# Partial shifts of the first convolution in tiles of 64 and 32 columns, with float32 weights laid out as a band

## Chip, core and metric

The kernel runs on one core of a Trainium2 chip. Every time here is in microseconds of that core (device time); a kernel is stated by the median of its runs. PE is TensorE (PEld its weight loads), DVE VectorE, ACT ScalarE, POOL GpSimd, SP the engine that issues most DMAs.

## What is computed

For 32 samples of 128 channels by 2048 positions the kernel applies four residual layers in float32. The first and the last are grouped convolutions (4 groups of 32 channels, 9 taps), the two between mix the channels with a matrix that depends on the sample.

```python
def _L0_cond_ref(x, c, weight, c_weight, bias):
    out = lax.conv_general_dilated(x, weight, window_strides=(STRIDE,), padding=[(PAD, PAD)],
                                   dimension_numbers=('NCH', 'OIH', 'NCH'), feature_group_count=GROUPS)
    ctx = jnp.einsum('nd,od->no', c, c_weight)
    out = out + ctx[:, :, None] + bias[None, :, None]
    return out
...
def _L1_cond_ref(x, embedding, W0, b0, W1, b1, W2, b2, weight, bias_k):
    ...
    att = jax.nn.softmax((h @ W2 + b2) / T, axis=-1)
    agg_w = jnp.einsum('bk,koi->boi', att, weight[..., 0])
    agg_b = att @ bias_k
    out = jnp.einsum('boi,bih->boh', agg_w, x) + agg_b[:, :, None]
    return out
...
x = x + _L0_cond_ref(x, cond_128, L0_cond_weight, L0_cond_c_weight, fside_S_0)
x = x + _L1_cond_ref(x, cond_128, ...)
x = x + _L2_cond_ref(x, cond_128, ...)
x = x + _L3_cond_ref(x, cond_128, L3_cond_weight, L3_cond_c_weight, fside_S_0)
```

## The kernel before

The 2048 positions of a sample are split into four phases (PH = 4, position modulo 4) of S = 512. For one group g, the 32 input channels stand in 32 partitions (`rows(g)`, one of PE's four row groups), and the four output phases times 32 output channels make 128 output columns of the array. With 9 taps and 4 phases there are SHIFTS = 12 shifts d. A shift reads phase `d % PH` of the input, moved by `d // PH` positions (`c`), and gives to output phase p the tap d - p, where that lies between 0 and 8. Six of the shifts (WHOLE, d = 3 to 8) reach all four phases. The other six (d = 0, 1, 2 and 9, 10, 11) reach some of them: the first three only the phases p <= d, the last three only the phases p > d - 9.

Float32 products come in two ways. The whole shifts are done in float32r, three times: high part of the taps by high part of x, low by high, high by low (`x_hi`, `x_lo`, `taps_hi`, `taps_lo`), each as a matmul of 32 rows by 128 columns that streams 512 columns of data (`whole_turns`, L1079). The partial shifts of samples 2 to 31 are done in plain float32, once, from `x_full` and `taps_raw`: `partial_turns` (L1090) makes three turns (PARTIAL = 3), n = 0, 1, 2. In a turn it issues for each group and each phase one tile of 32 rows by 32 columns: phase p takes shift n if p <= n, else shift n + 9. So d = n and d = n + 9 together fill the 128 columns, and a turn has 16 tiles, each at its own place of the array; PSUM bank g takes group g. Each float32 matmul is run by the chip in two passes. The first two samples use float32r for all shifts (`conv0`).

`conv0_mixed` is what a sample's first convolution is: whole turns with waits on `x_hi_done`, `x_lo_done` and the edges, for sample 2 also a product (`middle`), and then the partial turns. The last turn's matmuls count up `conv0_done` once a group; ScalarE (`high_y`, L639) and VectorE (`low_y`, L836) then take the banks. PE's order of work is written out by hand in `one`: the first convolution of sample b, the last convolution of sample b - 1 (L1068) with the small product for sample b + 1 (L1185, later L1192) in its midst, then the mix of sample b (L1214). The steady part is a loop of two samples a turn; 30 samples, 2 to 31, have partial turns.

`taps_raw[0]` is made by VectorE in the setup (L910, L913: a transpose, and the identity added for the residual), [channel of the group, tap, output channel]. `taps_raw_step[0]` reaches 2 when it is ready. GpSimd's program after the setup memsets is `spread_first` (two kinds of DMA issues, L560 and L563, which wait for the first product), `first_planes` (L527), and then one copy into phases of x (L496) and one weave of the output (L513) for each sample.

Of the kernel before, what the change touches and what calls it, by code (L numbers as in the profile page):

```python
# [30 lines left out]
N, C, L = 32, 128, 2048  # L31
G = 4
GC = C // G
# [10 lines left out]
WHOLE = [*range(PH, 2 * PH), PH - 1, 2 * PH]  # L44
PARTIAL = PH - 1
FIRST_MIXED = 2
K = 8
D = 128
DMA = 16
# [11 lines left out]
def conditioned_residual_kernel(nc, x, cond, side, conv0_w, ctx0_w, mix1, mix2, conv3_w, ctx3_w, out):  # L61
# [9 lines left out]
    with ctx:  # L71
        def sb(name, shape, dt=F32):
            return ctx.enter_context(nc.sbuf_tensor(name, shape, dt))
# [16 lines left out]

        taps_hi = [sb(f"taps_hi{l}", [C, SHIFTS, C], F32R) for l in range(2)]
        taps_lo = [sb(f"taps_lo{l}", [C, SHIFTS, C], F32R) for l in range(2)]
        mix1_w = sb("mix1_w", [C, K, C])
        mix2_wT = sb("mix2_wT", [C, K, C])
        mat1 = sb("mat1", [C, C])
# [71 lines left out]
        of_group_done = sem("of_group_done")  # L167
        taps_zeroed = [sem(f"taps_zeroed{l}") for l in range(2)]
        taps_raw_step = [sem(f"taps_raw_step{l}") for l in range(2)]
        taps_hi_done = [sem(f"taps_hi_done{l}") for l in range(2)]  # L170
        taps_lo_done = [sem(f"taps_lo_done{l}") for l in range(2)]
        mlp_rows_in = sem("mlp_rows_in")
# [315 lines left out]
        def _(pool):  # L488
# [91 lines left out]
                pool.memset(buf[:, :, ROW - 1:ROW].bitcast(F32), 0.0).then_inc(far_zeroed, 1)  # L580
            for buf in x_full:
                pool.memset(buf[:, :, 0:ROW:ROW - 1], 0.0).then_inc(far_zeroed, 1)
            spread_first()
            first_planes(ALL[1], 1)
            for t in ALL[2:N]:
# [474 lines left out]
        def _(pe):  # L1060
# [18 lines left out]
                        pe.matmul(ps[:, first_bank + g, :], w[rows(g), d, :], a[rows(g), d % PH, c:c + S],  # L1079
                                  start=(first and (k, d) == turns[0]), stop=False)  # L1080

            def partial_turns(first_bank, l, full, done, step):


                for n in range(PARTIAL):
                    for g in range(G):
                        for p in range(PH):
                            d = n if p <= n else n + TAPS
                            c = step * (d // PH)
                            tile = pe.matmul(ps[rows(p), first_bank + g, :], taps_raw[l][rows(g), d - p, :],  # L1090
                                             full[rows(g), d % PH, c:c + S], start=False, stop=(n == PARTIAL - 1))
                        if n == PARTIAL - 1:
                            tile.then_inc(done, 1)

            def conv0_mixed(t, middle=None):
                b = t.i
                hi, lo, full = x_hi[t.par(0)], x_lo[t.par(0)], x_full[t.par(0)]
                step = 1 if plain(t, 0) else BLK
                near, far = WHOLE[:PH], WHOLE[PH:]
                pe.wait_ge(x_hi_done, b + 1)  # L1100
                if t.at(N - 1):
                    pe.wait_ge(plain_ends, 3)
                wait(pe, out_act, 2 * (b - 1))
                wait(pe, out_dve, 2 * (b - 1))
                whole_turns(bank(t, 0), 0, hi, lo, [(k, d) for k in range(2) for d in near], step, True)
                if not plain(t, 0):
                    pe.wait_ge(x_hi_edged, b + 1 - PLAIN)
                whole_turns(bank(t, 0), 0, hi, lo, [(k, d) for k in range(2) for d in far], step, False)
                if not plain(t, 0):
                    pe.wait_ge(x_full_edged, b + 1 - PLANED)  # L1110
                pe.wait_ge(x_lo_done, b + 1)
                whole_turns(bank(t, 0), 0, hi, lo, [(2, d) for d in near], step, False)
                if not plain(t, 0):
                    pe.wait_ge(x_lo_edged, b + 1 - PLAIN)
                whole_turns(bank(t, 0), 0, hi, lo, [(2, d) for d in far], step, False)
                if middle:
                    middle()
                partial_turns(bank(t, 0), 0, full, conv0_done, step)

            def conv0(t, turns=range(TURNS)):  # L1120
                b = t.i
# [280 lines left out]
```

## Time and profile before

| | us |
|---|---|
| median of 3 runs | 632.58 (632.04 to 632.8) |
| profiled execution, its own time | 635.33 |
| its span, from the first to the last instruction | 633.5 |
| PE busy | 622.8 (98%) |
| DVE busy | 500.9 (79%) |
| ACT busy | 338.2 (53%) |
| POOL busy | 272.3 (43%) |

The profile is one execution. A busy time is the time in which an engine has at least one instruction in work; on PE several run at once in different places of the array, so that counts times durations exceed it. Ends of matmuls are modelled, their starts are read. The median above is of other executions than the profiled one.

### The profile page before, as it was taken

The page shows a single profiled execution, that of the slowest core. Times are in us where ns is not written, and L with a number is a line of the kernel's source. Part 1 is how long each engine was busy: PE and PEld are TensorE (multiplying, and loading weights), DVE is VectorE, ACT ScalarE, POOL GpSimd, SP SyncE. Part 2 cuts the span into 40 slices and gives each one's busy share as a digit, 9 for nine tenths or more (in the row PEclk, how much of TensorE's full clock was granted, in tenths as well). Part 3 has the DMA queues.
Part 4 walks back from the last instruction along what each step waited for, and adds up shares of the span by engine and source line. Part 5 has one row for each costly group of instructions (what it writes and reads, how often), then busy time and mean ns, then how long its engine had stood idle before and what let it go on. Part 6 is the DMA issues. An engine that isn't in the chain of part 4 may idle for free.

```text
span 633.5 us, 26750 instructions
## 1 busy us (share of the span) xinstructions
PE 622.8 (98%) x11938; PEld 506.3 (80%) x11938; DVE 500.9 (79%) x1002; ACT 338.2 (53%) x626; POOL 272.3 (43%) x163
## 2 busy tenths in 40 slices
PE   8999999999999999999999999999999999999995
PEld 6888897777788777889877778777878877788874
DVE  6899777978777887887887887797877788788735
ACT  4665455555455456455456446555545545645534
POOL 4133454354355345355435345435435534534220
PEclk8999999999999999999999999999999999999998
DMA  8066665557765556775555776555776555655515
GB/s 244 24 188 215 203 211 177 204 163 225 232 207 156 190 176 199 232 232 158 173 191 175 232 232 182 158 202 162 223 232 208 155 190 176 201 169 168 161 76 201
DMA packets 50572, 118.84 MB, mean 188 GB/s; under 512 B 5621, under 2 KB 26282, under 8 KB 42714
## 3 DMA queue, kind: packets, MB, share of 16 engines
q1 hardware_dynamic: 49170, 116.04, 58.1%
q0 software_dynamic: 576, 1.26, 0.5%
q10 hardware_dynamic: 776, 0.89, 0.4%
q8 instruction: 30, 0.49, 0.3%
q14 instruction: 20, 0.16, 0.1%
HBM read 35.33 MB, written 33.55 MB: 109 GB/s over the span
## 4 chain that ended last, share of the span: by engine, by line
PE 96%; DMA 2%; DVE 1%; ACT 1%; issue 0%; ACTq 0%; DVEq 0%
PE ps L1068 45%; PE ps L1079 19%; PE ps L1090 16%; PE ps L1214 14%; PE ps L1192 1%; DMA out_sb<-in_L_cond_weight 1%; DMA out_planes<-out_taps 1%; ACT out_sb L740 1%; PE ps L1262 0%; PE ps L1185 0%; DVE out_taps L856 0%; DVE x_in L950 0%; DVE x_hi L993 0%; PE ps L1250 0%; PE ps L1302 0%
## 5 line engine op out<-in xcount | busy, mean ns | idle before, releaser
L513 POOL COPY out_sb<-out_planes 128x2048 f32<-128x2048 f32 x30 | 123.0, 4099 | 187.8 <-issue 162.0
L496 POOL COPY x_full<-x_in 128x2048 f32<-128x2048 f32 x29 | 117.1, 4038 | 113.9 <-DVE x_lo L822 110.1
L846 DVE SCALAR_TENSOR_TENSOR z_lo<-ps,bias_tab,z_hi 128x1024 fp32r<-128x1024 f32 x62 | 76.7, 1279 | 60.7 <-ACT z_hi L649 60.7
L1090 PE MATMUL ps<-x_full,taps_raw 32*32 32x512 f32 x2880 | 102.2, 598 | 0.0
L1068 PEld LDWEIGHTS ps<-z_hi,taps_hi 32*128 32x128 f32 x1488 | 71.0, 183 | 35.4 <-issue 25.1
L1068 PE MATMUL ps<-z_hi,taps_lo 32*128 32x512 f32 x1488 | 96.5, 387 | 0.0
L836 DVE SCALAR_TENSOR_TENSOR y_lo<-ps,bias_tab,y_hi 128x512 fp32r<-128x512 f32 x128 | 87.2, 744 | 10.2 <-ACT y_hi L639 10.2
L1068 PE MATMUL ps<-z_hi,taps_hi 32*128 32x512 f32 x1488 | 94.2, 396 | 0.0
L657 ACT ACTIVATE out_taps<-ps,bias_tab 128x512 f32<-128x512 f32 x62 | 39.3, 685 | 102.2 <-PE ps L1068 102.2
L1068 PE MATMUL ps<-z_lo,taps_hi 32*128 32x512 f32 x1488 | 90.3, 385 | 0.0
L1214 PE MATMUL ps<-y_hi,mix_w 32*128 32x512 f32 x1024 | 88.0, 385 | 0.0
L649 ACT ACTIVATE z_hi<-ps,bias_tab 128x1024 fp32r<-128x1024 f32 x62 | 65.8, 1113 | 34.2 <-PE ps L1214 34.2
L1068 PEld LDWEIGHTS ps<-z_lo,taps_hi 32*128 32x128 f32 x1488 | 77.9, 183 | 6.9
L639 ACT ACTIVATE y_hi<-ps,bias_tab 128x512 fp32r<-128x512 f32 x128 | 77.0, 683 | 9.9 <-PE ps L1090 7.6
L1068 PEld LDWEIGHTS ps<-z_hi,taps_lo 32*128 32x128 f32 x1488 | 75.1, 183 | 6.1
L1090 PEld LDWEIGHTS ps<-x_full,taps_raw 32*32 32x32 f32 x2880 | 42.1, 103 | 43.2 <-issue 35.6
L822 DVE TENSOR_TENSOR x_lo<-x_full,x_hi 128x2048 fp32r<-128x2048 f32 x31 | 70.8, 2284 | 0.0
L601 ACT ACTIVATE x_hi<-x_full 128x2048 fp32r<-128x2048 f32 x30 | 57.9, 1931 | 2.0 <-POOL x_full L527 2.0
L898 DVE TENSOR_REDUCE prod_sum<-ps 128x128 f32<-128x1024 f32 (+2 forms) x31 | 35.4, 1143 | 29.3 <-PE ps L1192 24.3
L1214 PEld LDWEIGHTS ps<-y_hi,mix_w 32*128 32x128 f32 x1024 | 53.9, 183 | 4.7 <-DVE y_lo L836 0.3
L691 ACT ACTIVATE mat_hi<-mat 128x128 fp32r<-128x128 f32 x27 | 8.4, 311 | 91.1 <-DVE mat L875 91.1
L1214 PE MATMUL ps<-y_lo,mix_w 32*128 32x512 f32 x512 | 52.9, 385 | 0.0
(158 smaller groups left out, 831.0 us busy)
## 6 DMA issues: line engine op xcount, KB each, us to landing
x_in<-in_x SPq DMA_DIRECT2D x31, 1024.0 KB, 5.3
out_planes<-out_taps SPq DMA_DIRECT2D x122, 256.0 KB, 3.6
out<-out_sb SPq DMA_DIRECT2D x30, 1024.0 KB, 4.6
mix_w<-prod SPq DMA_DIRECT2D x124, 128.0 KB, 4.0
x_in<-in_x SPq DMA_DIRECT2D x2, 512.0 KB, 5.9
out<-out_sb POOLq DMA_DIRECT2D x2, 512.0 KB, 3.5
out<-x_full SPq DMA_DIRECT2D x7, 128.0 KB, 2.9
out_taps<-in_L_cond_weight SPq DMA_DIRECT2D x1, 512.0 KB, 5.8
```

The costliest lines, as they stand in the source:

```text
L496: pool.tensor_copy(row_order(t, d, x[:, :, home(t, d)]), x_order(t, d, x_in[t.par(d)][:, :])).then_inc(x_planed, 1)
L513: pool.tensor_copy(x_order(t, d, out_sb[t.par(d)][:, :]), row_order(t, d, out_planes[:, :, :]))\
L601: act.activation(x_hi[p][:, :, home(t, d)], x_full[p][:, :, home(t, d)], ACT.Copy).then_inc(x_hi_done, 1)
L639: act.activation(y_hi[:, g, :], ps[:, bank(t, 0) + g, :], ACT.Identity, bias=bias_tab[:, b, g:g + 1]).then_inc(y_hi_done, 1)
L649: act.activation(z_home(t, 0)[0][:, 2 * h:2 * h + 2, home(t, 0)], ps[:, k:k + 2, :], ACT.Identity, bias=bias_tab[:, b, 2 * G:BIAS]).then_i ...
L822: dve.tensor_tensor(out=x_lo[p][:, :, home(t, d)], in0=x_full[p][:, :, home(t, d)], in1=x_hi[p][:, :, home(t, d)].bitcast(F32), op=ALU.sub ...
L836: dve.scalar_tensor_tensor(out=y_lo[:, g, :], in0=ps[:, bank(t, 0) + g, :], scalar=bias_tab[:, b, g:g + 1], in1=y_hi[:, g, :].bitcast(F32) ...
L846: dve.scalar_tensor_tensor(out=z_home(t, 0)[1][:, 2 * h:2 * h + 2, home(t, 0)], in0=ps[:, k:k + 2, :], scalar=bias_tab[:, b, 2 * G:BIAS], ...
L1068: tile = pe.matmul(ps[:, first_bank + g, :], w[rows(g), d, :], a[rows(g), d % PH, c:c + S], start=(n == 0), stop=(n == TURNS - 1))
L1079: pe.matmul(ps[:, first_bank + g, :], w[rows(g), d, :], a[rows(g), d % PH, c:c + S], start=(first and (k, d) == turns[0]), stop=False)
L1090: tile = pe.matmul(ps[rows(p), first_bank + g, :], taps_raw[l][rows(g), d - p, :], full[rows(g), d % PH, c:c + S], start=False, stop=(n == ...
L1214: tile = pe.matmul(ps[:, bank(t, 0) + p, :], w[rows(p), g, h, :], a[rows(p), g, :], start=(n == 0), stop=(n == 3 * G - 1))
```

## The change

`TILES` lists for each turn the tiles as (shift, first phase, end phase). Neighbouring phases that take the same shift are joined where two of them make a tile of 64 columns that starts at column 0 or 64; the others stay at 32 columns. With four groups a turn has 12, 8 and 12 matmuls instead of 16 each. A tile of 64 columns needs the taps of both phases side by side: `taps_full` holds, for each of the six partial shifts, the 128 columns with the taps of the phases that the shift reaches and zeros elsewhere. GpSimd fills it once, with a memset and six copies, behind its setup memsets; PE waits for it ahead of sample 2.

```diff
+TILES = (((0, 0, 1), (9, 1, 2), (9, 2, 4)), ((1, 0, 2), (10, 2, 4)), ((2, 0, 2), (2, 2, 3), (11, 3, 4)))
...
+            pool.memset(taps_full[:, :, :], 0.0).then_inc(taps_full_zeroed, 1)
+            pool.wait_ge(taps_full_zeroed, 1)
+            pool.wait_ge(taps_raw_step[0], 2)
+            for p in range(PH):
+                if p < PARTIAL:
+                    last = pool.tensor_copy(taps_full[:, p:PARTIAL, rows(p)], taps_raw[0][:, 0:PARTIAL - p, :])
+                if p > 0:
+                    last = pool.tensor_copy(taps_full[:, PARTIAL:PARTIAL + p, rows(p)], taps_raw[0][:, TAPS - p:TAPS, :])
+            last.then_inc(taps_full_done, 1)
             spread_first()
...
-                for n in range(PARTIAL):
+                for n, tiles in enumerate(TILES):
                     for g in range(G):
-                        for p in range(PH):
-                            d = n if p <= n else n + TAPS
-                            c = step * (d // PH)
-                            tile = pe.matmul(ps[rows(p), first_bank + g, :], taps_raw[l][rows(g), d - p, :],
-                                             full[rows(g), d % PH, c:c + S], start=False, stop=(n == PARTIAL - 1))
-                        if n == PARTIAL - 1:
+                        for d, p, q in tiles:
+                            c, o = step * (d // PH), slice(GC * p, GC * q)
+                            tile = pe.matmul(ps[o, first_bank + g, :], taps_full[rows(g), d if d < PARTIAL else d - TAPS + PARTIAL, o],
+                                             full[rows(g), d % PH, c:c + S], start=False, stop=(n == len(TILES) - 1))
+                        if n == len(TILES) - 1:
                             tile.then_inc(done, 1)
...
+                if t.at(FIRST_MIXED):
+                    pe.wait_ge(taps_full_done, 1)
```

PE's order at the partial turns of sample 2, before the change. A row is a run of like matmuls with the columns of the array by the columns streamed, and their count:

```order
L1079 MATMUL ps<-x_lo,taps_hi 128x512 x24
L1185 MATMUL ps<-mat2T,mat 128x128 x4
L1090 MATMUL ps<-x_full,taps_raw 32x512 x48
L1068 MATMUL ps<-z_hi,taps_hi 128x512 x48
L1068 MATMUL ps<-z_hi,taps_lo 128x512 x40
```

The same place of the changed program (L1092, L1199, L1102 and L1081 are the lines that were L1079, L1185, L1090 and L1068):

```order
L1092 MATMUL ps<-x_lo,taps_hi 128x512 x24
L1199 MATMUL ps<-mat2T,mat 128x128 x4
L1102 MATMUL ps<-x_full,taps_full 32x512 x2
L1102 MATMUL ps<-x_full,taps_full 64x512
...
L1102 MATMUL ps<-x_full,taps_full 32x512 x2
L1102 MATMUL ps<-x_full,taps_full 64x512 x10
L1102 MATMUL ps<-x_full,taps_full 32x512 x2
L1102 MATMUL ps<-x_full,taps_full 64x512
...
L1102 MATMUL ps<-x_full,taps_full 32x512 x2
L1081 MATMUL ps<-z_hi,taps_hi 128x512 x48
```

One run of 48 tiles of one size has become 15 runs that alternate between 32 and 64 columns (eight of two tiles, six of one, one of ten), and this is so for each of the 30 samples.

GpSimd's order in the setup, before the change, with the waits named:

```order
L582 MEMSET x_full 128x4x2 x2
L560 DMA mix_w<-prod 32x4x128 [waits prod_hi_done]
L563 DMA mix_w<-prod 32x4x128 [waits prod_lo_done]
L563 DMA mix_w<-prod 32x4x128
L527 COPY x_full<-x_in 128x4x8x32 [waits x_lo_done,z_hi_done,x_hi_done,x_loaded0]
```

And in the changed program:

```order
L586 MEMSET x_full 128x4x2 x2
L587 MEMSET taps_full 128x768
L592 COPY taps_full<-taps_raw 128x3x32 [waits taps_raw_step0,taps_full_zeroed]
L592 COPY taps_full<-taps_raw 128x2x32
L594 COPY taps_full<-taps_raw 128x32
L592 COPY taps_full<-taps_raw 128x32
L594 COPY taps_full<-taps_raw 128x2x32
L594 COPY taps_full<-taps_raw 128x3x32
L564 DMA mix_w<-prod 32x4x128 [waits prod_hi_done]
```

The memset and the six copies stand ahead of the first DMA issue that waits for the product.

## Rows read from the trace of the kernel before

**Rows 1.** The page: busy time of each engine, granted TensorE clock in 40 slices
```profile
PE 622.8 (98%) x11938; PEld 506.3 (80%) x11938; DVE 500.9 (79%) x1002; ACT 338.2 (53%) x626; POOL 272.3 (43%) x163
...
PEclk8999999999999999999999999999999999999998
```

**Rows 2.** The page: chain that ended last, shares of the span by line
```profile
PE ps L1068 45%; PE ps L1079 19%; PE ps L1090 16%; PE ps L1214 14%; PE ps L1192 1%; DMA out_sb<-in_L_cond_weight 1%; DMA out_planes<-out_taps 1%; ACT out_sb L740 1%; PE ps L1262 0%; PE ps L1185 0%; DVE out_taps L856 0%; DVE x_in L950 0%; DVE x_hi L993 0%; PE ps L1250 0%; PE ps L1302 0%
```

**Rows 3.** That chain from 290 to 345: by line; start, us, what
```profile
by line: PE ps L1068 43.9%; PE ps L1079 22.2%; PE ps L1090 18.2%; PE ps L1214 14.8%; PE ps L1192 1.3%
...
301.51 3.33 PE ps L1090 x91
...
320.33 3.33 PE ps L1090 x91
```

**Rows 4.** Groups by line and shape, PE: rows*columns, count | busy us, mean ns
```profile
L1090 PE MATMUL ps<-x_full,taps_raw 32*32 32x512 f32 x2880 | 102.2, 598 | 0.0
...
L1068 PE MATMUL ps<-z_lo,taps_hi 32*128 32x512 f32 x1488 | 90.3, 385 | 0.0
```

**Rows 5.** Timeline around 301.4: start, us, engine, line, shapes, count [idle before]
```profile
301.13 0.38 PE L1079 MATMUL ps<-x_lo,taps_hi 32*128 32x512 f32 x1
...
301.44 0.24 PEld L1090 LDWEIGHTS ps<-x_full,taps_raw 32*32 32x32 f32 x32 [0.35 <-issue]
```

**Rows 6.** Timeline within the stretch: five short windows between 302.1 and 303.9
```profile
301.90 0.69 PE L1090 MATMUL ps<-x_full,taps_raw 32*32 32x512 f32 x16
...
302.33 0.89 PE L1090 MATMUL ps<-x_full,taps_raw 32*32 32x512 f32 x7
...
302.33 0.37 PEld L1090 LDWEIGHTS ps<-x_full,taps_raw 32*32 32x32 f32 x11 [0.32 <-issue]
...
302.52 0.18 PEld L1090 LDWEIGHTS ps<-x_full,taps_raw 32*32 32x32 f32 x10
...
303.20 1.22 PE L1090 MATMUL ps<-x_full,taps_raw 32*32 32x512 f32 x17
```

**Rows 7.** Timeline around 304.8, where the stretch ends
```profile
304.05 0.81 PE L1090 MATMUL ps<-x_full,taps_raw 32*32 32x512 f32 x14
...
304.26 0.59 PE L1090 MATMUL ps<-x_full,taps_raw 32*32 32x512 f32 x1
304.78 0.50 PE L1068 MATMUL ps<-z_hi,taps_hi 32*128 32x512 f32 x4
...
304.78 0.30 PEld L1068 LDWEIGHTS ps<-z_hi,taps_hi 32*128 32x128 f32 x8 [0.84 <-issue]
```

**Rows 8.** Timeline around 56.3, first such stretch, behind the product
```profile
56.04 0.27 PE L1185 MATMUL ps<-mat2T,mat 32*128 32x128 f32 x1
56.24 0.70 PE L1090 MATMUL ps<-x_full,taps_raw 32*32 32x512 f32 x14
```

**Rows 9.** Timeline around 83.9, float32 product and float32r convolution, one size
```profile
83.85 0.53 PEld L1068 LDWEIGHTS ps<-z_hi,taps_lo 32*128 32x128 f32 x9
...
83.88 0.28 PE L1185 MATMUL ps<-mat2T,mat 32*128 32x128 f32 x3
```

**Rows 10.** Timeline of POOL, 0 to 62
```profile
0.74 0.52 POOL L540 MEMSET y_hi<- 128x512 f32 x1 [0.29 <-POOLq L1388]
...
28.56 0.58 POOL L560 DMA_DIRECT2D mix_w<-prod  x1 [21.17 <-DVE prod L901]
...
45.14 0.79 POOL L531 COPY x_full<-x_full 128x189 f32<-128x189 f32 x2
```

**Rows 11.** The chain in order of time, near its start
```profile
8.31 1.10 DVE x_hi L993
```

**Rows 12.** Windows: stretch, length, busy us (count) PE PEld DVE ACT POOL, clock, DMA
```profile
6.00:8.00 2.00, 1.10 (x4) 0.62 (x4) 1.50 (x3) 0.76 (x4) 1.39 (x11) 1.00 1.05 310
...
11.00:12.00 1.00, 1.00 (x13) 0.84 (x16) 0.90 (x3) 0.87 (x3) 0.00 (x0) 0.57 1.23 352
...
17.00:18.00 1.00, 1.00 (x20) 0.91 (x16) 0.28 (x1) 0.00 (x0) 0.00 (x0) 0.52 0.08 16
```

More of the change, by code:

```diff
@@ L92, in conditioned_residual_kernel @@
         taps_lo = [sb(f"taps_lo{l}", [C, SHIFTS, C], F32R) for l in range(2)]
+        taps_full = sb("taps_full", [C, 2 * PARTIAL, C])
         mix1_w = sb("mix1_w", [C, K, C])
@@ L169, in conditioned_residual_kernel @@
         taps_raw_step = [sem(f"taps_raw_step{l}") for l in range(2)]
+        taps_full_done = sem("taps_full_done")
+        taps_full_zeroed = sem("taps_full_zeroed")
         taps_hi_done = [sem(f"taps_hi_done{l}") for l in range(2)]
@@ L1080, in whole_turns, with partial_turns @@
                                   start=(first and (k, d) == turns[0]), stop=False)
-            def partial_turns(first_bank, l, full, done, step):
-                for n in range(PARTIAL):
+            def partial_turns(first_bank, full, done, step):
+                for n, tiles in enumerate(TILES):
                     for g in range(G):
-                        for p in range(PH):
-                            d = n if p <= n else n + TAPS
-                            c = step * (d // PH)
-                            tile = pe.matmul(ps[rows(p), first_bank + g, :], taps_raw[l][rows(g), d - p, :],
-                                             full[rows(g), d % PH, c:c + S], start=False, stop=(n == PARTIAL - 1))
-                        if n == PARTIAL - 1:
+                        for d, p, q in tiles:
[3 more added lines that the diff above has]
+                        if n == len(TILES) - 1:
                             tile.then_inc(done, 1)
@@ L1117, in conv0_mixed @@
                     middle()
-                partial_turns(bank(t, 0), 0, full, conv0_done, step)
+                partial_turns(bank(t, 0), full, conv0_done, step)
             def conv0(t, turns=range(TURNS)):
```

## Prediction

> **What bounds the kernel now.** I read the page's busy times first: TensorE (PE) is busy 622.8 of 633.5 us, VectorE 500.9, ScalarE 338.2, GpSimd 272.3, and the clock granted to PE stands at 9 tenths or more in all but the first and the last slice [rows 1]. In the chain of work that ended last, the five heaviest lines are all PE's and hold 95%; the one that the change rewrites, L1090, holds 16% [rows 2]. So one sample costs what PE needs for it. The chain in order of time gives the period: L1090 starts at 301.51 and again at 320.33, 18.82 us apart, with 3.33 us on L1090, and no other engine has a piece in that part of the chain [rows 3]. There are 30 such stretches, one for each sample from the third on: 2880 matmul records of 96 each [rows 4]. The program has 48 matmuls of 32 rows by 32 columns there; each float32 matmul leaves two records (two passes over its 512 columns), each with its weight load.
>
> **How one stretch is made up now.** From the first weight load at 301.44 to the next line's first at 304.78 it takes 3.34 us [rows 5, 7]. A tile's two passes stand one behind the other, sixteen tiles side by side: the second passes start at 301.90, 0.46 us after the first ones, and the first tile of the next turn follows at 302.33, 0.43 us later [rows 5, 6]. So a pass streams for 0.43 us, and 0.03 more shows where a load of 32 columns has nothing to hide behind. Six passes are 2.56 us; the rest of the 3.34 is two pauses at the turns of the loop (one is the 0.19 us between the loads of 302.33 and 302.52 [rows 6]), the staggered issue, and the changes of tile size at the ends.
>
> **Those changes of tile size decide this case.** Ahead of the stretch the last 128-column matmul starts at 301.13. Its 512 columns take 0.21 us, half of 0.43 (one pass of float32r), so it has streamed by 301.34, and the first load of 32 columns comes only at 301.44: 0.10 us of nothing, and PE's load side idle for 0.35 us [rows 5]. Behind it the last 32-column matmul starts at 304.26 and has streamed by 304.69; the first load of 128 columns comes at 304.78, 0.09 later, and all four row groups start together [rows 7], although the last round of matmuls had begun at 304.05 with row group 0, some 0.2 us before its last one. So PE waits for its whole array there, not for the rows that it needs. A third case: a 128-column matmul of 128 streamed columns starts at 56.04, ends by 56.15, and the 32-column tiles start at 56.24 [rows 8]. That it is the size and not the type of the data, the change from float32 to float32r at one size tells: the next line's loads start at 83.85, while the last product matmuls are still running until 84.16 [rows 9]. The trace has no step between 32 and 64 columns; both its ends (128 to 32, 32 to 128) cost the same wait. The Trainium skill, "TensorEngine Tiling (Array Packing)", section "Key Properties", says that changing the tiling mode, and not just the tile, drains TensorE; it lists 32x32 and 32x64 as different modes. By that rule the trace's two waits are such drains, and this change has many more; by a reading in which only the step to and from full width drains, the sum below would be that of the second rival.
>
> **What is removed.** 16 of 48 matmuls a sample, that is 32 of 96 pairs of load and pass. None of this shortens the six passes that a tile place needs in three turns: the tiles were side by side already. The most that can be gained is 3.34 less six passes, one bare load and one drain (2.56 + 0.03 + 0.09 = 2.68): 0.66 us a sample, 20 us in all.
>
> **What is added on PE.** The order of the new program changes size inside the stretch: two tiles of 32 columns, one of 64, and so on. Between two changes stands a run; there are 15: eight pairs of 32 columns, six single tiles of 64, and one run of ten tiles of 64 (the last of turn 0, the eight of turn 1, the first of turn 2). If each change lets the array run empty, a run costs its whole length, since nothing of the next can start beside it:
> - a pair of 32 columns: 0.46 to the second pass, 0.43 for that, 0.09 for the drain = 0.98 us. The second tile of the pair starts a hundredth later and is in the rounding. Eight: 7.84 us.
> - a single tile of 64: the bare load is between 0.03 (32 columns) and 0.11 (128 columns: passes right behind a drain last 0.50 against 0.39 [rows 4, 7]); I take 0.05, in proportion. 0.05 + 2 x 0.43 + 0.09 = 1.00 us. Six: 6.00 us.
> - the run of ten: two of its places are used twice, so four passes in a row: at least 0.05 + 4 x 0.43 + 0.09 = 1.86 us. At most what two full turns take now, from 301.44 to the last second pass at 303.20 [rows 6], plus 0.43 and 0.09 = 2.28. I take 2.1, since fewer tiles are queued but their order is much like today's.
>
> Sum 15.94 us instead of 3.34: +12.6 a sample, on the path, as PE is the chain. Times 30: +378 us. Nothing covers it: PE waits for no engine there. Nothing of it is given back either, since what follows on PE (L1068, the product, the mix) is bound by PE itself [rows 3]. The other engines get more slack, DVE at 501 of then some 1010 us. ScalarE takes over a bank when its group's last matmul is done; these now end one row group after another, 2 us apart, long before the mix needs them.
>
> **The band of weights.** GpSimd gets a memset of 768 elements (one of 512 takes 0.52 us, so 0.8) and six copies of 32 to 96 elements, 0.2 to 0.4 us each by the copies of 189 (0.79 for two): 2 to 3 us in all. They stand in the 21.17 us in which GpSimd idles ahead of the DMA issue of 28.56 [rows 10]; the wait for taps_raw ends before the cast of x_hi that VectorE starts behind it [rows 11]. Queued behind them on GpSimd are the spread of the first mix weights and the first planes, all long after. PE's new wait comes at its third sample, near 52 us. Both cost 0. What is not free for certain is VectorE beside those copies: 1.10 us of that cast, from 8.31, are on the chain. I bound that by 0 and 1 us and take 0.
>
> **Total.** The profiled execution has a span of 633.5 us (635.33 by its own time) against a median of 632.58; its stretches are counted in its own time, and the difference of 2.8 us is carried along. 632.6 + 378 = 1010.6, so 1010 us (the span: 1011).
>
> **Range of this case.** If the run of ten is at its bounds and a drain 0.09 to 0.10, the stretch is 15.6 to 16.3 us, 1000 to 1022. If each change also brings a pause like that of 0.19 us at a turn [rows 6], 14 x 0.19 = 2.7 more a sample, 81 in all: 1090. Below, if a few loads can slip forward, 0.05 a run: 985.
>
> **Rival 1: the clock falls too.** In such a run one or two tiles of sixteen places work (two to four 32-column places), where now all do. In this trace the granted clock fell from 2.4 to 1.2 GHz at about 11.1 us and stayed there to 18.0, although PE was full again by then; before it, from 6 to 8 us, PE was busy for 1.10 of 2.00 us, with four matmuls [rows 12]. Against it: with streams 87% of the time a run is no idle stretch, and the clock held through all 30 dense stretches. What thin tiles count for, no row shows. Its price: at half clock a run has 0.88 us more, fourteen of them 12.3, the run of ten 1.8; and as the clock took 6.9 us to return (11.1 to 18.0), up to 3.4 us behind. Up to 17.5 a sample; about half of it if the clock falls midway: 1010 + 30 x 8.8 = 1274 us (at most 1540).
>
> **Rival 2, on the other side: 32 and 64 columns run side by side.** Then row group g's pair and its 64-column tile start as the four tiles do now. From which point it decides: whether a load of 64 columns starts within 0.02 us of the 32-column one before it, or 0.9 behind it. For it: the observed drains both involve full width, so the trace leaves it open; the places of the tiles do not overlap. Against it: the wait seen is for the whole array, even for row groups long free, as a setting of the array and not of a tile would be. The Trainium skill, "TensorE: Matmul & The Clock Gate", section "Part 3: Packing small matmuls", has tiles at different positions run at once and 16 of them cost little over one; the trace agrees for one size (sixteen second passes within 0.69 us [rows 6]). Time: a third less issued, the two pauses (0.5 us of the 0.66) perhaps halved: -0.3 a sample, 623 us; at best 613, at worst 633 if the pauses are no matter of count.
>
> **How the numbers follow.** Forecast (every change drains, clock stays) 0.68; rival 1 0.12; rival 2 with a gain 0.16, with none 0.04. One can tell about 0.2% (1.3 us) from no change here. So faster 0.16, same 0.04, slower 0.80. The range is to hold 0.8: the forecast's own 985 to 1090 holds 0.65, so it must reach to one side. Rival 2 weighs more than rival 1, and a partial drain would lie between, so it runs from 612 to 1090, and leaves rival 1 out.
>
> **What would show it.** Right: L1102 (the new line) takes 15 to 17 us from its first load to L1081's first, its loads come in 15 groups about 1 us apart, and PE's load side idles 0.9 us before most of them; passes stay at 0.59 us and the granted clock at full; the period is 31.4 us. Rival 1 shows as passes of over 1 us and a granted clock of 0.5 in and behind the stretch. Rival 2 shows as 12, 8 and 12 tiles within tenths of a microsecond, and a stretch under 3.34. Wrong by size: drains of over 0.2 us, or a run of ten over 2.3.

## Result, and the profile after

| kernel | median us | runs |
|---|---|---|
| before | 632.58 | 632.04 to 632.8 |
| changed | 1378.60 | 1378.15 to 1378.83 |

The ratio is 2.180 (95% interval 2.175 to 2.185). The prediction said 1010 us, 612 to 1090: the direction is right, the size is 369 us short, and the time lies outside the range. The profiled execution of the changed kernel is the one of 1378.6 us, its span 1376.8.

The page of the changed kernel, busy times, granted clock in 40 slices, and the line of partial turns (now L1102):

```profile
PE 1367.3 (99%) x10978; PEld 620.3 (45%) x10978; DVE 509.8 (37%) x1002; ACT 350.5 (25%) x626; POOL 264.0 (19%) x170
...
PEclk9876677766776667766777667776677667776677
...
L1102 PE MATMUL ps<-x_full,taps_full 32*32 32x512 f32 (+1 forms) x1920 | 788.0, 978 | 0.0
```

Against [rows 1] and [rows 4]: a third of the matmul records is gone (2880 to 1920), PE is still the bound, and yet these 1920 are busy for 788.0 us instead of 102.2, with 978 ns of a pass instead of 598. The granted clock, which stood at 9 tenths in all slices but two, is at 6 or 7 in nearly all.

The chain in order of time (start, us, what), one sample from stretch to stretch, to hold beside [rows 3]:

```profile
620.75 25.96 PE ps L1102 x64
646.71 7.38 PE ps L1081 x71
654.08 0.24 PE ps L1206 x8
654.32 3.64 PE ps L1081 x63
657.96 2.72 PE ps L1228 x48
660.68 4.08 PE ps L1092 x72
664.76 25.61 PE ps L1102 x64
690.37 6.12 PE ps L1081 x66
```

The period is 44.0 us instead of 18.82. The stretch takes 25.96 instead of 3.33 (+22.6), the piece behind it 7.38 instead of some 4.8 (+2.6), and the rest is as before. (Some samples are shorter: the mean period is 43.7 us, some 24.9 more than before, and thirty of these make the 746 us measured.)

What a run of tiles costs shows in PE's loads. At the start of one stretch, clock at 2.4 GHz (start, us, what [idle time of the load side before it]):

```profile
664.69 0.14 PEld L1102 LDWEIGHTS ps<-x_full,taps_full 32*32 32x32 f32 x4 [0.35 <-issue]
665.67 0.19 PEld L1102 LDWEIGHTS ps<-x_full,taps_full 32*64 32x64 f32 x2 [0.84 <-issue]
666.67 0.14 PEld L1102 LDWEIGHTS ps<-x_full,taps_full 32*32 32x32 f32 x4 [0.81 <-issue]
667.64 0.19 PEld L1102 LDWEIGHTS ps<-x_full,taps_full 32*64 32x64 f32 x2 [0.84 <-issue]
```

0.98 us for a pair of 32 columns (664.69 to 665.67), 1.00 for a single tile of 64 (to 666.67), 0.97 again: the forecast's terms to the hundredth, and the load side idle for 0.8 us before each change. Later in the same stretch:

```profile
673.63 0.33 PEld L1102 LDWEIGHTS ps<-x_full,taps_full 32*64 32x64 f32 x16 [1.66 <-issue]
...
677.23 0.18 PEld L1102 LDWEIGHTS ps<-x_full,taps_full 32*32 32x32 f32 x4 [1.61 <-issue]
679.08 0.28 PEld L1102 LDWEIGHTS ps<-x_full,taps_full 32*64 32x64 f32 x2 [1.66 <-issue]
680.97 0.18 PEld L1102 LDWEIGHTS ps<-x_full,taps_full 32*32 32x32 f32 x4 [1.61 <-issue]
```

A pair now takes 1.85 us, a single tile 1.89, and the run of ten 3.60. It stands at the lower clock in every sample; what such a run takes at 2.4 GHz, the run of twelve in `halves` below shows: 1.89 us, near the 1.86 that the forecast had as its least. Between the two pieces the clock fell, as the windows show (length, busy us with counts of PE PEld DVE ACT POOL, granted clock, DMA share, GB/s):

```profile
664.70:669.30 4.60, 4.60 (x20) 0.78 (x16) 4.26 (x17) 0.93 (x4) 0.00 (x0) 1.00 0.49 199
669.30:690.40 21.10, 21.10 (x54) 2.94 (x52) 2.36 (x4) 2.06 (x3) 3.68 (x1) 0.50 0.12 50
690.40:693.20 2.80, 2.80 (x28) 2.24 (x32) 0.75 (x1) 2.75 (x4) 0.00 (x0) 0.50 0.00 0
693.20:697.00 3.80, 3.80 (x76) 3.31 (x72) 0.16 (x1) 0.14 (x1) 0.00 (x0) 1.00 0.00 0
```

A granted clock of 1.00 is 2.4 GHz, 0.50 is 1.2 GHz. 4.6 us into the stretch PE goes to the lower level; it stays there for the other 21.1 us of the stretch and for 2.8 us of the dense work behind it. This repeats with every sample: in all 30 stretches the clock falls, 3.1 to 5.2 us after their start. So there are two causes one on top of the other: the runs stand one behind the other, and their work does not hold the clock. The experiments take them apart.

### The profile page after: what moved, and what is told of

It reads as the page before. It is cut to its first block, busy times and chain, and to the rows that moved or that the text cites. A ratio compares the mean times of both kernels' runs of the same rounds, so it can differ in the third digit from the quotient of the medians.

```text
span 1376.8 us, 24839 instructions
## 1 busy us (share of the span) xinstructions
PE 1367.3 (99%) x10978; PEld 620.3 (45%) x10978; DVE 509.8 (37%) x1002; ACT 350.5 (25%) x626; POOL 264.0 (19%) x170
## 4 chain that ended last, share of the span: by engine, by line
PE 98%; ACT 0%; DMA 0%; DVE 0%; issue 0%; ACTq 0%; POOL 0%; DVEq 0%; POOLq 0%
PE ps L1102 57%; PE ps L1081 25%; PE ps L1092 9%; PE ps L1228 6%; PE ps L1330 0%; PE ps L1206 0%; DMA out_planes<-out_taps 0%; ACT out_sb L753 0%; PE ps L1276 0%; ACT L787 0%; DVE out_taps L869 0%; DVE x_in L963 0%; PE ps L1264 0%; PE ps L1303 0%; PE ps L1199 0%
## 5 line engine op out<-in xcount | busy, mean ns | idle before, releaser
L1102 PE MATMUL ps<-x_full,taps_full 32*32 32x512 f32 (+1 forms) x1920 | 788.0, 978 | 0.0
L1102 PEld LDWEIGHTS ps<-x_full,taps_full 32*32 32x32 f32 (+1 forms) x1920 | 109.5, 159 | 636.9 <-issue 636.7
L849 DVE SCALAR_TENSOR_TENSOR y_lo<-ps,bias_tab,y_hi 128x512 fp32r<-128x512 f32 x128 | 95.5, 750 | 605.4 <-ACT y_hi L652 605.4
L652 ACT ACTIVATE y_hi<-ps,bias_tab 128x512 fp32r<-128x512 f32 x128 | 87.3, 687 | 611.6 <-PE ps L1102 609.3
L1081 PE MATMUL ps<-z_hi,taps_hi 32*128 32x512 f32 x1488 | 153.7, 585 | 0.0
L517 POOL COPY out_sb<-out_planes 128x2048 f32<-128x2048 f32 x30 | 110.5, 3682 | 196.3 <-issue 161.8
L1081 PEld LDWEIGHTS ps<-z_hi,taps_hi 32*128 32x128 f32 x1488 | 111.7, 301 | 76.0 <-issue 49.9
L1081 PE MATMUL ps<-z_hi,taps_lo 32*128 32x512 f32 x1488 | 97.9, 391 | 0.0
L1081 PE MATMUL ps<-z_lo,taps_hi 32*128 32x512 f32 x1488 | 90.5, 385 | 0.0
L1081 PEld LDWEIGHTS ps<-z_lo,taps_hi 32*128 32x128 f32 x1488 | 79.7, 183 | 5.3
L1081 PEld LDWEIGHTS ps<-z_hi,taps_lo 32*128 32x128 f32 x1488 | 76.0, 189 | 9.8
L1092 PE MATMUL ps<-x_hi,taps_lo 32*128 32x512 f32 x720 | 52.4, 385 | 0.0
```

The source lines that it names most:

```text
L517: pool.tensor_copy(x_order(t, d, out_sb[t.par(d)][:, :]), row_order(t, d, out_planes[:, :, :]))\
L652: act.activation(y_hi[:, g, :], ps[:, bank(t, 0) + g, :], ACT.Identity, bias=bias_tab[:, b, g:g + 1]).then_inc(y_hi_done, 1)
L849: dve.scalar_tensor_tensor(out=y_lo[:, g, :], in0=ps[:, bank(t, 0) + g, :], scalar=bias_tab[:, b, g:g + 1], in1=y_hi[:, g, :].bitcast(F32) ...
L1081: tile = pe.matmul(ps[:, first_bank + g, :], w[rows(g), d, :], a[rows(g), d % PH, c:c + S], start=(n == 0), stop=(n == TURNS - 1))
L1102: tile = pe.matmul(ps[o, first_bank + g, :], taps_full[rows(g), d if d < PARTIAL else d - TAPS + PARTIAL, o], full[rows(g), d % PH, c:c + ...
```

## The experiments

All take the changed kernel's band of weights and GpSimd's work for it. But for `sizes_32_late`, which also moves GpSimd's work, they differ in the table of runs only: a run is a choice of row groups and, for each, a list of tiles (shift, first phase, end phase). The common loop is

```diff
-                for n, tiles in enumerate(TILES):
-                    for g in range(G):
+                for n, (groups, tiles) in enumerate(RUNS_OF):
+                    for g in groups:
                         for d, p, q in tiles:
```

and each `diff` below gives `RUNS_OF`, shortened by names for its parts; A stands for `range(G)`. (Left out: the flag and the semaphore that mark the last matmul of a bank go with the last run that writes it.) Behind "Measured" stand the median, the ratio to the kernel before on the same chip with its 95% interval, and as "clock" the mean granted share of 2.4 GHz over the profiled execution. `dense_changes`, `halves_long` and the five named `thin_...` add tiles to the sum, so that it is not the convolution's; their times are read for the work on PE alone. In the profiles of these kernels the partial tiles are L1100, the convolutions L1092 and L1081 and the mix L1233.

### One change of size

```diff
+RUNS_OF = ((A, ((0, 0, 1), (9, 1, 2), (2, 2, 3), (11, 3, 4))), (A, ((2, 0, 2), (9, 2, 4))), (A, ((1, 0, 2), (10, 2, 4))))
```

> The same 32 tiles a sample as the changed kernel, with the band weights, in another order: first all sixteen of 32 columns (they fill the sixteen places), then the sixteen of 64. One change of size inside the stretch instead of fourteen. Theory (each change of size lets the array run empty, and only that made the changed kernel's runs serial): a run of sixteen 32s 0.98 us, a run of 64s with two turns 1.86 to 2.28, stretch 2.84 to 3.26 instead of 3.34 of before: 617 to 630 us, clock full. Rival (tiles of 64 columns are slow or thin for the clock in themselves): stretch well over 3.34, granted clock under 0.9, over 700 us.

Measured: 627.21 us (626.65 to 627.91), ratio to before 0.992 (0.990 to 0.994), clock 0.995. The same 32 tiles, the same weights, and it takes 0.8% less than before, a small gain that is clear of the noise, and less than half the time of the changed kernel. Its loads:

```profile
297.41 0.24 PEld L1100 LDWEIGHTS ps<-x_full,taps_full 32*32 32x32 f32 x32 [0.35 <-issue]
298.49 0.28 PEld L1100 LDWEIGHTS ps<-x_full,taps_full 32*64 32x64 f32 x16 [0.84 <-issue]
298.97 0.23 PEld L1100 LDWEIGHTS ps<-x_full,taps_full 32*64 32x64 f32 x8 [0.20 <-issue]
299.40 0.23 PEld L1100 LDWEIGHTS ps<-x_full,taps_full 32*64 32x64 f32 x8 [0.20 <-issue]
300.44 0.30 PEld L1081 LDWEIGHTS ps<-z_hi,taps_hi 32*128 32x128 f32 x8 [0.81 <-issue]
```

1.08 us for sixteen tiles of 32 columns and 1.95 for sixteen of 64 in two turns, 3.03 together. A run of one pair costs 0.98, a run of sixteen 1.08: the tiles are all but free, the run is what is paid. The 64-column tiles are not slow in themselves. And between the two turns of 64s there is no pause like that of before [rows 6]: the loads of one pass follow those of the pass before by 0.43 us.

The stretch is 0.31 us shorter than before, which would be 9.3 us in 30 samples, but the kernel gains 5.0. `band_32` below accounts for some 0.8 us. Another part is a wait that the kernel before does not have, of PE's loads for the small product (L1211) on VectorE (waited for: us in total, times, longest):

```profile
PEld ps L1211 <- DVE y_lo L849: 5.6, 24, 0.3
```

From the stretch's end to the product's end it is now 4.90 us instead of 4.79, so 0.11 of the 0.31 us is given back. PE is no longer the only bound here.

### The same tiles turn by turn, and by halves

```diff
+# turns_grouped
+RUNS_OF = ((A, ((0, 0, 1), (9, 1, 2))), (A, ((9, 2, 4),)), (A, ((1, 0, 2), (10, 2, 4))), (A, ((2, 0, 2),)), (A, ((2, 2, 3), (11, 3, 4))))
+# halves: L = range(2), U = range(2, G)
+RUNS_OF = ((L, ((0, 0, 1), (9, 1, 2))), (L, ((9, 2, 4),)), (U, ((0, 0, 1), (9, 1, 2))), (U, ((9, 2, 4),)),
+           (A, ((1, 0, 2), (10, 2, 4))), (L, ((2, 0, 2),)), (L, ((2, 2, 3), (11, 3, 4))), (U, ((2, 0, 2),)), (U, ((2, 2, 3), (11, 3, 4))))
```

> The same tiles, turn by turn as in the changed kernel, but within turns 0 and 2 the 32s of all groups together: runs of 8, 16 and 8 tiles, two changes of size inside the stretch. Theory (run length sets the time): 0.98 + (1.86 to 2.28) + 0.98 = 3.8 to 4.2 us, 647 to 660 us, clock full. Rival (64-column tiles are the trouble): as in the run before, far above.

> The same tiles, in turns 0 and 2 alternating by halves of the groups: runs of 4, 2, 4, 12, 4, 2, 4 tiles, six changes of size inside the stretch. Length theory: 6 x 0.98 to 1.00 + 1.86 = 7.8 us, +4.4 a sample, 765 us with the clock at full. If the clock falls wherever PE has few places at work, this stretch too is followed by 1.2 GHz and the time is 850 to 950 us; if only stretches as long as those of the changed kernel (16 us) bring it down, the clock stays full.

Measured: turns_grouped 650.30 us (650.16 to 650.8), ratio 1.029 (1.027 to 1.030), a stretch of 3.96 us; halves 767.60 us, ratio 1.217 (1.213 to 1.221), a stretch of 7.85 us, clock 0.997. With one, two, six changes of size inside the stretch it takes 3.03, 3.96 and 7.85 us, each as counted from the length of its runs. The chain of turns_grouped, that of halves, and the loads of the run of twelve in halves with those behind it:

```profile
305.92 3.96 PE ps L1100 x64
```

```profile
309.83 7.85 PE ps L1100 x64
317.68 4.80 PE ps L1081 x75
```

```profile
312.74 0.24 PEld L1100 LDWEIGHTS ps<-x_full,taps_full 32*64 32x64 f32 x16 [0.84 <-issue]
...
314.63 0.15 PEld L1100 LDWEIGHTS ps<-x_full,taps_full 32*32 32x32 f32 x8 [0.81 <-issue]
```

The clock stayed at full here, and the piece behind the stretch has its 4.80 us. So the serial runs are one cause, shown by itself. The expectation's "if the clock falls wherever PE has few places at work" did not come true.

### The band alone

```diff
+RUNS_OF = ((A, ((0, 0, 1), (9, 1, 2), (9, 2, 3), (9, 3, 4))), (A, ((1, 0, 1), (1, 1, 2), (10, 2, 3), (10, 3, 4))), (A, ((2, 0, 1), (2, 1, 2), (2, 2, 3), (11, 3, 4))))
```

> Only the band of weights and GpSimd's work for it are taken over: 48 tiles of 32 columns in the order of before, read from the band. Theory (the band costs nothing): 632.6 us within 0.3%. Rival (the band's weights or GpSimd's copies beside VectorE's cast of x_hi cost in the setup): up to 1 us more, and more if a load of weights from the band is slower.

Measured: 632.94 us (632.54 to 633.42), ratio 1.0013 (1.0003 to 1.0023), the stretch 3.34 us as before. The band costs nothing in a stretch. Over the whole kernel it is 0.8 us more (0.2 to 1.5 by the interval), within the 1 us of the expectation's rival; where that lies, no run shows.

### Is it the changes or the thin work that brings the clock down?

```diff
+# dense_changes: T = ((0, 0, 1), (9, 1, 2), (2, 2, 3), (11, 3, 4)), W = ((2, 0, 2), (9, 2, 4))
+RUNS_OF = ((A, T), (A, W)) * 7 + ((A, T),)
+# thin_one_size: B is the table of band_32
+RUNS_OF = ((range(1), ((0, 0, 1), (9, 1, 2)) * 14),) + B
+# thin_four_places
+RUNS_OF = ((range(1), ((0, 0, 1), (9, 1, 2), (9, 2, 3), (9, 3, 4)) * 14),) + B
```

> As many changes of size as the changed kernel has, but with every run wide: fifteen runs a sample, eight of sixteen tiles of 32 columns and seven of eight tiles of 64, all sixteen places busy in each (the sums are then not the convolution's: tiles are added several times). Runs of sixteen 32s took 1.08 us in the run with one change; 8 x 1.08 + 7 x 1.07 = 16.1 us a stretch, +12.8 a sample. Theory A (few places at work bring the clock down, not the changes): clock full, 1016 us. Theory B (the repeated emptying of the array brings it down): granted clock near 0.7, 1350 us or more.

> No change of size but thin work: ahead of a stretch of 48 tiles of 32 columns as before, 28 more in the same size, all in two places of row group 0 (they are added to the sum, which is not the convolution's then). The passes of a place run one behind the other without a gap: 28 x 0.427 = 12.0 us. Theory A (thin work alone brings the clock down): it falls 4 to 5 us into each stretch and time is 1200 to 1350 us. Theory B (it takes the changes and their gaps): clock full, 632 + 360 = 992 us.

> As thin_one_size, but the added tiles fill all four column places of row group 0 (56 more tiles, 28 passes one behind the other in each place, the same 12.0 us; the sum is not the convolution's). If the number of places at work is what counts, and four are enough as in the run by halves: clock full, 992 us, whatever the run with two places does. If one row group of four is too thin: 1200 us or more.

Measured: dense_changes 1068.82 us, clock 0.983; thin_one_size 1370.21 us, clock 0.746; thin_four_places 1344.39 us, clock 0.759. Windows of 3, 3 and 6 us from the start of a stretch, of dense_changes, thin_one_size and thin_four_places in turn:

```profile
420.90:423.90 3.00, 3.00 (x84) 0.76 (x80) 3.00 (x13) 0.41 (x2) 0.00 (x0) 1.00 0.73 303
423.90:426.90 3.00, 3.00 (x80) 0.81 (x64) 1.35 (x6) 0.51 (x2) 1.18 (x1) 1.00 0.00 0
426.90:432.90 6.00, 6.00 (x150) 1.35 (x136) 0.00 (x0) 0.00 (x0) 2.60 (x1) 1.00 0.38 156
```

```profile
135.90:138.90 3.00, 3.00 (x19) 0.78 (x18) 3.00 (x13) 0.37 (x2) 0.00 (x0) 1.00 0.81 329
138.90:141.90 3.00, 3.00 (x14) 0.73 (x12) 1.31 (x6) 0.51 (x2) 1.24 (x1) 0.85 0.02 8
141.90:147.90 6.00, 6.00 (x17) 1.31 (x15) 0.00 (x0) 0.00 (x0) 2.48 (x1) 0.50 0.39 162
```

```profile
134.30:137.30 3.00, 3.00 (x34) 0.87 (x34) 3.00 (x13) 0.38 (x2) 0.00 (x0) 1.00 0.89 330
137.30:140.30 3.00, 3.00 (x28) 0.80 (x24) 1.31 (x6) 0.51 (x2) 1.20 (x1) 0.72 0.04 16
140.30:146.30 6.00, 6.00 (x36) 1.48 (x32) 0.00 (x0) 0.00 (x0) 2.53 (x1) 0.50 0.38 156
```

Fourteen changes of size a sample with wide runs keep the clock through a stretch of 16.27 us; passes without any change or gap, in one row group, lose it in all 30 stretches, 2.7 to 5.9 us after their start. Theory A holds as against B: the emptying of the array does not bring the clock down. But four places fell as two did, while halves has four places at work too. So the number of places does not decide.

dense_changes came out 53 us above its count, and thin_one_size 20 us above its range. dense_changes has a stretch of 16.27 us for the 16.1 expected (5 us in all) and something new, PE idle at its first convolution for 28.7 us in 11 pieces; that, and the short falls of the clock that go with it, is the rest of its 53 us. thin_one_size has such idle time too, 51.7 us in 22 pieces, more than the 20 us above its range. These waits are told in the last section.

### Turn 0 alone

```diff
+# S(g) = ((range(g, g + 1), ((0, 0, 1), (9, 1, 2))), (range(g, g + 1), ((9, 2, 4),)))
+RUNS_OF = S(0) + S(1) + S(2) + S(3) + ((A, ((1, 0, 2), (10, 2, 4))), (A, ((2, 0, 2),)), (A, ((2, 2, 3), (11, 3, 4))))
```

> Turn 0 as in the changed kernel (runs of 2, 1, 2, 1, 2, 1, 2 tiles), the rest grouped (runs of 13 and 8). At full clock 4 x 0.98 + 3 x 1.00 + 1.9 + 1.03 = 9.85 us, +6.5 a sample, 827 us. If thin work is what counts, its 7 us of one and two tiles bring the clock down in most samples (in the changed kernel it fell 3.6 to 5.1 us into the stretch), while the 7.85 us of two and four tiles in the run by halves did not: 950 to 1100 us. If the length of the whole stretch counts and lies between 7.85 and 16 us: open, clock full or not in all samples alike.

Measured: 956.11 us, ratio 1.513 (1.508 to 1.517), clock 0.853. The clock fell in all 30 stretches, 3.4 to 5.2 us in. One of them took 14.66 us instead of the 9.85 of full clock:

```profile
408.41 14.66 PE ps L1100 x64
```

One row group at a time for 7 us is enough; it need not be the changed kernel's 16.

### Length, places, or row groups?

```diff
+# thin_two_groups
+RUNS_OF = ((range(2), ((0, 0, 1), (9, 1, 2)) * 14),) + B
+# thin_two_groups_b
+RUNS_OF = ((range(2), ((0, 0, 1), (9, 1, 2))),) * 14 + B
+# halves_long: H is the first four runs of halves, R the other five
+RUNS_OF = H * 3 + R
+# thin_two_rows_one_column
+RUNS_OF = ((range(2), ((0, 0, 1),)),) * 14 + B
```

> As thin_four_places, but the four places are columns 0 to 63 of row groups 0 and 1, those that the run by halves used (56 more tiles of one size, 12.0 us; the sum is not the convolution's). If the run by halves kept its clock because its places spread over two row groups: clock full, near 1040 us (992 and the pauses at the loop's turn seen in the other two). If it kept it because its thin pieces were short (3 us, with a wide run between): the clock falls within 3 to 5 us as in the other two, 1340 us or more.

This run did not test what it was meant to. The loop over row groups stands outside the list, so all 28 tiles of row group 0 came ahead of those of row group 1. Had the two groups run side by side, the stretch would have 12.0 and 3.34 us; one after the other it has 24 and 3.34 at full clock. It took 43.99 us, with the clock down in all 30 stretches:

```profile
429.63 43.99 PE ps L1100 x208
```

The kernel took 1957.46 us with a clock of 0.681. It is one more case of one row group at a time. The next one has the order that was meant.

> 28 passes one behind the other in four places at once (columns 0 to 63 of row groups 0 and 1), no change of size, 12.0 us more than before (the sum is not the convolution's). Clock full: 992 us and some 40 us of pauses at the loop's turn. Clock down as in the run with four places of one row group: about 1340 us.

> The run by halves with its alternating turn 0 three times instead of once (runs of 4, 2, 4, 2 tiles; the sum is not the convolution's): 8 runs more of 0.98 us, a stretch of 15.7 us at full clock, about as long as the changed kernel's would have been (15.9). If halves kept its clock by its wider runs: clock full, 767.6 + 30 x 7.9 = 1004 us. If by its length: the clock falls 4 to 8 us into the stretch, 1250 to 1400 us.

> 28 passes one behind the other in two places at once, column place 0 of row groups 0 and 1, no change of size, 12.0 us more than before (the sum is not the convolution's). If it is the row groups at work that tell: clock full as with four places of two row groups, 1030 to 1050 us. If it is the places: clock down as with two places of one row group, 1340 to 1370 us.

Measured: thin_two_groups_b 1050.74 us, clock 0.977; halves_long 1009.13 us, clock 0.995; thin_two_rows_one_column 1082.57 us, clock 0.958. Windows of thin_two_groups_b and of halves_long from the start of a stretch:

```profile
145.50:148.50 3.00, 3.00 (x32) 0.88 (x32) 3.00 (x13) 0.39 (x2) 0.00 (x0) 1.00 0.72 302
148.50:151.50 3.00, 3.00 (x32) 0.88 (x28) 1.33 (x6) 0.51 (x2) 1.22 (x1) 1.00 0.01 3
151.50:157.50 6.00, 6.00 (x77) 2.07 (x74) 0.00 (x0) 0.00 (x0) 2.53 (x1) 1.00 0.37 149
```

```profile
401.40:404.40 3.00, 3.00 (x24) 0.50 (x20) 3.00 (x13) 0.42 (x2) 0.00 (x0) 1.00 0.69 289
404.40:407.40 3.00, 3.00 (x20) 0.54 (x16) 1.36 (x6) 0.51 (x2) 1.18 (x1) 1.00 0.00 0
407.40:413.40 6.00, 6.00 (x54) 1.35 (x56) 0.00 (x0) 0.00 (x0) 2.52 (x1) 1.00 0.37 153
```

and the chain of thin_two_rows_one_column, two stretches in a row:

```profile
393.45 15.35 PE ps L1100 x146
...
424.27 15.35 PE ps L1100 x146
```

15.35 us is 12.0 and 3.34: no passes at the lower level. halves_long has a stretch of 15.83 us, the length that the changed kernel's would have at full clock (15.7 to 15.9), and its time is within 0.5% of the 1004 us expected for full clock. All cases in one table (for the five `thin_...` kernels the row is of the added tiles, ahead of their 3.34 us with all places at work):

| kernel | row groups at work at once | places at once | changes of size | clock in the stretch |
|---|---|---|---|---|
| changed | 1 (4 in the run of ten) | 2 | 14 | falls in 30 of 30 |
| one_turn | 1 for 7 us | 2 | 8 | falls in 30 of 30 |
| thin_one_size | 1 | 2 | 0 | falls in 30 of 30 |
| thin_two_groups | 1 | 2 | 0 | falls in 30 of 30 |
| thin_four_places | 1 | 4 | 0 | falls in 30 of 30 |
| thin_two_rows_one_column | 2 | 2 | 0 | holds in all 30 |
| thin_two_groups_b | 2 | 4 | 0 | holds in all 30 |
| halves, halves_long | 2 (4 in the run of twelve) | 4 | 6, 14 | holds in all 30 |
| dense_changes | 4 | 16 | 14 | holds in all 30 |

With two places, the same count of passes and the same duration of a stretch at full clock (thin_one_size and thin_two_rows_one_column), the clock fell when both stood in one row group and held when they stood in two. It is neither the places, nor the length, nor the changes. What it is about one row group stays open: in all these kernels a row group also has its own quarter of the input's partitions and its own PSUM bank, so that one row group is also one bank written at a time, and no run separates them.

### Order of the two sizes, and a later band

```diff
+# sizes_64_first
+RUNS_OF = ((A, ((1, 0, 2), (10, 2, 4))), (A, ((2, 0, 2), (9, 2, 4))), (A, ((0, 0, 1), (9, 1, 2), (2, 2, 3), (11, 3, 4))))
+# sizes_32_late: sizes_32_first, and on GpSimd
+            spread_first()
+            first_planes(ALL[1], 1)
             pool.memset(taps_full[:, :, :], 0.0).then_inc(taps_full_zeroed, 1)
...
             last.then_inc(taps_full_done, 1)
-            spread_first()
-            first_planes(ALL[1], 1)
```

> The order with one change of size again, beside the two below on one chip: stretch 3.03 us as measured (1.08 for sixteen 32s, 1.95 for two turns of 64s), 626 to 628 us.

> The same two runs in the other order, 64s first. If only the number and the length of the runs count: 3.03 us a stretch, 626 to 628 us. If the first run's loads matter (64 columns bare instead of 32) or what follows: up to 0.05 us a sample, 1.5 us more.

> As sizes_32_first, with GpSimd's band built behind the first planes instead of ahead of them, so that nothing of GpSimd runs beside VectorE's cast of x_hi and the work behind it. In the profile of sizes_32_first the casts took 2.83 us instead of 2.10. Theory (the two engines hinder each other there, on the chain of the setup): 0.7 to 1.2 us less than sizes_32_first, 625.5 to 626.5. Rival (the setup is not on the path, or GpSimd's later work starts late): no difference, or slower.

Measured against 632.37 of before on the same chip: sizes_32_first_again 626.88 us (ratio 0.992, 0.990 to 0.993), sizes_64_first 626.69 (0.991, 0.989 to 0.992), sizes_32_late 626.89 (0.991, 0.990 to 0.993). The three can't be told apart. The order of the sizes is free, as the count by runs says. The theory of the setup fell: in one profile of sizes_32_first VectorE's casts of x_hi took 2.83 us, but in the repeat 2.11 and in before 2.10 (its part on the chain stands in [rows 11]), and moving GpSimd's work away gained nothing. sizes_64_first has the wait for VectorE as well, 5.5 us in 24 pieces. 626.7 us is the best time of this study, 0.9% under before.

## Why the prediction was wrong, and what in it was right

**What bounds the kernel, and that nothing covers an increase:** right. PE is 99% busy, and every microsecond of the stretch went to the period. (Towards shorter stretches this ends soon: in sizes_32_first VectorE's y_lo took back 0.11 of 0.31 us.)

**A change between 32 and 64 columns lets the whole array run empty** (the forecast's mechanism): right, and now shown: 0.98 and 1.00 us a run, 15 runs, and with one, two and six changes the times of 627, 650 and 768 us. The Trainium skill, "TensorEngine Tiling (Array Packing)", section "Key Properties", says that a change of the tiling mode drains TensorE; these runs agree, for a change of the column size alone. The second rival, tiles of both sizes side by side, is refuted; its point of decision, the next load 0.9 us behind, came out on the forecast's side (0.98).

**The terms:** 0.98 for the pairs and 1.00 for the single tiles measured 0.97 to 0.98 and 1.00. The run of ten was taken at 2.1; the run of twelve in halves, also four passes deep, took 1.89. So the stretch would be 15.7 us instead of 15.94, and at full clock the kernel would take some 1004 us (an estimate: 632.6 and 30 times 12.4). halves_long, with a stretch of 15.83 us and a full clock, took 1009.13.

**The step that failed is the clock.** The forecast kept it at 2.4 GHz and gave its fall a chance of 0.12, "with streams 87% of the time a run is no idle stretch, and the clock held through all 30 dense stretches". The busy share was the wrong thing to look at: thin_one_size streams without a gap and loses the clock all the same. And the dense stretches of before spoke for nothing here, since in all of them four row groups work; the changed kernel's runs have one. What the runs showed in place of a full clock: it fell in all 30 stretches, 3.1 to 5.2 us after their start, and that makes 375 of the 746 us (1378.6 less 1004). The Trainium skill, "TensorE: Matmul & The Clock Gate", section "What's actually happening", says that the gate goes by how busy PE has been recently. By PE's busy time in the profile (100% of the windows above) it should have stayed open, and it did not; for such work the measurement decides.

**The price of the first rival** was sized too low as well. Its 0.88 us a run at half clock is right (1.85 less 0.98 is 0.87), and its upper end of 1540 held. But its middle, +8.8 us a sample, took the clock to fall midway. It fell 3.1 to 5.2 us into a stretch of 15.7, so two thirds of the work or more ran at the lower level, about 10 us more, and 1.3 or 2.6 us came behind (6.12 and 7.38 us for the piece of 4.8): 12.5 a sample on average, a period of 43.7 us. That is 1378.6 instead of 1274. The range was drawn to the second rival (0.20) and left the first (0.12) out; the two were weighed by what the trace showed of sizes, and the trace showed nothing of one row group at work.

**The band** was put at 0 us, with 1 as its bound: band_32 measured 0.8, so inside the bound and without weight here. What was to show the forecast right (groups of loads about 1 us apart, with the load side idle before them) is there while the clock is full, with 0.8 us idle for the 0.9 forecast; "passes stay at 0.59 us" is not, with a median of 1.06.

## What to carry to other kernels

When tiles of different size are mixed, order them by size first where the dependencies allow it: the same 32 matmuls took 1378.6 us alternating by row group and 626.7 us in two runs. Price a change of tile size as the whole time of the run before it, since nothing of the next size starts beside it, and fill every run with tiles of all row groups. When the stretch on PE has become shorter, look for the next engine in its waits: here VectorE took back a third of the gain. And where a change leaves PE with one row group at work for several microseconds, take the lower clock as the likely case, however full PE's busy time looks.

## What the runs showed of the chip beyond that

- A change of size waits 0.09 us from the end of the streams to the next load at 2.4 GHz ([rows 7], and the same between 32 and 64 columns), so the price of a change is small where runs are long, and the run's own 0.9 us where they are short.
- With one row group of 32 rows at work the granted clock fell to 1.2 GHz within 2.7 to 5.9 us in every stretch of the five kernels that had it; with two row groups, in two places only, it stayed at 2.4 GHz in the stretches.
- Loops with a long body pause. In dense_changes, thin_one_size, thin_four_places, thin_two_groups, thin_two_groups_b and thin_two_rows_one_column PE stood still for up to 3.3 us ahead of the first convolution of a sample, and sometimes within it, waiting for nothing that the profile shows; before, and halves_long with 12418 matmul records, have no such wait. The waits of thin_two_rows_one_column (13618 records; "issue" is time in which PE waited for nothing that the profile shows; us in total, times, longest):

```profile
PE ps L1092 <- issue: 52.9, 22, 3.3
```

The clock falls for 3.4 to 10 us around many of these pauses, which is why dense_changes, thin_two_groups_b and thin_two_rows_one_column have 0.983, 0.977 and 0.958 although their stretches run at full clock. The pauses belong to the loop over pairs of samples: it is passed twelve times, so it turns eleven times, and each of the six kernels has its pauses at eleven places, two samples apart, all at the first convolution with which the loop's body begins. Between 12418 records (none) and 13618 (all eleven) lies the step; whether the fetching of a longer loop body is behind it was not tried.
